# Narrow attention of two stages: unrolled program, value products of two units together, first loads issued one phase earlier

## The reference

```python
# causal, per sequence b and head h, 8 features a head, L = 1024
scores = einsum('bhqd,bhkd->bhqk', q, k) / sqrt(8)
scores = where(causal, scores, -inf)
probs  = softmax(scores, axis=-1)
o      = einsum('bhqk,bhkd->bhqd', probs, v)

# encoder block: no mask, no scaling; the bias enters outside the softmax
att     = softmax(einsum('nqd,nkd->nqk', qm, km), axis=-1)
att_out = einsum('nqk,nkd->nqd', att + batch_pos, vm)
```

## Time and profile before

| | us |
|---|---|
| three executions | 2846.60, 2834.06, 2837.32 |
| median | 2837.32 |
| the profiled execution, its own time | 2839.78 |
| its span in the trace | 2837.9 |

### The profile page before, as it was taken

The page is one execution under the profiler, slowest core; times in us unless marked ns, Lnnn a source line. Parts: engine busy times, 40 slices in busy tenths (PEclk is TensorE's granted clock), DMA queues, the critical chain, the costliest instruction groups (busy, mean ns, idle before and its releaser), DMA issues. The chain is left out here.

```text
span 2837.9 us, 41505 instructions
## 1 busy us (share of the span) xinstructions
PE 2460.7 (87%) x12171; PEld 1456.0 (51%) x12236; DVE 2092.1 (74%) x4150; ACT 1431.1 (50%) x3040; POOL 616.5 (22%) x605
## 2 busy tenths in 40 slices
PE   6994989949988999789996499999848899969998
PEld 4773344327756555467773422222225555437776
DVE  4984777538968999279995088788437899739998
ACT  3552456615522777146664026666711377616665
POOL 2324001013326000124444100000003400013443
PEclk7996899969979999789996669999978999979999
DMA  1213232022212000034432621211033000004443
GB/s 64 83 54 80 51 66 58 13 55 88 76 38 49 1 1 1 8 130 142 156 138 48 153 46 28 54 29 29 5 48 82 5 1 1 8 9 156 149 149 118
DMA packets 110480, 175.28 MB, mean 62 GB/s; under 512 B 58739, under 2 KB 81139, under 8 KB 98467
## 3 DMA queue, kind: packets, MB, share of 16 engines
q1 hardware_dynamic: 93428, 171.23, 20.6%
q10 hardware_dynamic: 16896, 2.10, 0.5%
HBM read 145.43 MB, written 12.78 MB: 56 GB/s over the span
## 5 line engine op out<-in xcount | busy, mean ns | idle before, releaser
L1543 DVE TENSOR_REDUCE b1x_maxima<-b1x_m_bank 128x1 f32<-128x512 f32 x512 | 318.1, 684 | 85.7 <-PE b1x_m_bank L1461 85.6
L1583 ACT ACTIVATE b1x_probs<-b1x_e_bank 128x1024 f32<-128x1024 f32 x256 | 248.4, 1021 | 119.9 <-PE b1x_e_bank L1479 111.6
L1543 DVE TENSOR_REDUCE a1x_maxima<-a1x_m_bank 128x1 f32<-128x512 f32 (+3 forms) x384 | 190.1, 551 | 72.6 <-PE a1x_m_bank L1464 48.6
L1461 PE MATMUL b1x_m_bank<-b1a_k_slot,b1a_q_slot 96*128 96x512 bf16 x512 | 191.4, 414 | 21.2 <-DMA b1x_v_slot<-b1a_v_aug 20.1
L1583 ACT ACTIVATE a1x_probs<-a1x_e_bank 128x1024 f32<-128x1024 f32 (+1 forms) x192 | 147.5, 809 | 103.4 <-PE a1x_e_bank L1482 80.1
L1479 PE MATMUL b1x_e_bank<-b1a_q_slot,b1a_k_slot 128*128 128x512 bf16 x475 | 146.7, 387 | 8.3 <-issue 4.3
L1495 PE MATMUL b1x_o_bank<-b1x_probs,b1x_v_slot 128*32 128x512 f32 x1024 | 138.8, 614 | 0.7 <-ACT b1x_probs L1583 0.7
L1461 PE MATMUL a1x_m_bank<-a1a_k_slot,a1a_q_slot 96*128 96x512 bf16 (+3 forms) x384 | 120.5, 352 | 18.3 <-DMA a1x_v_slot<-a1a_v_aug 16.7
L1461 PEld LDWEIGHTS b1x_m_bank<-b1a_k_slot,b1a_q_slot 96*128 96x128 bf16 x512 | 41.7, 98 | 180.5 <-DVE b1x_maxima L1543 130.9
L632 ACT ACTIVATE g2e_high<-g2e_hidden 128x512 fp32r<-128x512 f32 x128 | 81.1, 633 | 91.7 <-DVE g2e_hidden L665 91.5
L632 ACT ACTIVATE g1e_high<-g1e_hidden 128x512 fp32r<-128x512 f32 x128 | 81.1, 633 | 91.0 <-DVE g1e_hidden L665 91.0
(11 more groups left out here) (567 smaller groups left out, 6624.6 us busy)
## 6 DMA issues: line engine op xcount, KB each, us to landing
g1e_share<-scratch_combine SPq DMA_DIRECT2D x32, 1024.0 KB, 4.9
g2e_share<-scratch_combine SPq DMA_DIRECT2D x32, 1024.0 KB, 4.8
f1e_share<-scratch_combine SPq DMA_DIRECT2D x9, 1024.0 KB, 4.8
f2e_share<-scratch_combine SPq DMA_DIRECT2D x9, 1024.0 KB, 4.9
b1e_window<-scratch_bias_table SPq DMA_DIRECT2D x16, 320.0 KB, 4.7
a1a_k_slot<-scratch_k_parts SPq DMA_DIRECT2D x24, 192.0 KB
a1a_q_slot<-scratch_q_parts SPq DMA_DIRECT2D x72, 64.0 KB
b1a_k_slot<-scratch_k_parts SPq DMA_DIRECT2D x24, 192.0 KB
```

Of the source, the lines that this page charges most:

```text
L1461: mm = pe.matmul(bank[:, 0:width], q_slot[s][0:MAX_ROW, qt // 4, hh, chunk(qt % 4, 128)], k_slot[s][0:MAX_ROW, hh, k0:k0 + width], start=T ...
L1543: dve.tensor_reduce(maxima[:, k0 // NC, col:col + 1], bank[:, 0:width], AX, ALU.max).then_inc(m_taken, 1)
L1583: act.activation(probs[g % 2][:, 2 * pair:2 * pair + 2, 0:width], e_bank[pair][:, :, 0:width], ACT.Exp, scale=scale).then_inc(exp_done, 1)
```

## The change

Five things change, in both attentions.

1. **No loops.** Every engine's program of the attention phase is written out for all 8 groups (16 query halves). The units of all groups form one list (`units`), the items another (`items`).
2. **Order on PE.** For every two units u and u+1: the four score pairs of units u+2 and u+3, an item behind each of them, a fifth item, then the value products of u and of u+1 together, then the rest of the items. `probs` has four buffers instead of two; there are still two `e_bank` and three `m_bank`.
3. **Lead and shares.** Items are dealt out by their width (`worth`, `due`) and evenly over all units, with a fixed lead: 68 items stand before the first scores in `a1x` (before: 50) and 53 in `b1x` (before: 66, turns counted). A turn stands four items behind the last maximum of its half. In `b1x` the 58 rounds with items hold 8, 8, 8 and 9 of them in turn (the last of the 58 holds 5) and 6 rounds hold none; in `a1x` a group's six rounds hold 10, 5, 10, 12, 9 and 4, and the last 8 of 48 rounds none.
4. **Loads.** Group 0 is loaded by SP in the phase before (`narrow_values`, and in `relative_bias` behind the windows' loads). A group is loaded by 6 transfers: a query part is one transfer with a broadcast source to its three places. The values are read from `v_aug` where they lie, without the copy `v_slot`. Groups 1 and 2 are both loaded at the start of the attention, ahead of the first `rows`.
5. **POOL.** The third part of the maxima is written by the subtraction itself, so a half takes four POOL instructions instead of five.

The diff, cut to its core:

```diff
+    def load(self, sp, group):
+        n, s = group * 4, group % SLOTS
+        for i in range(PARTS):
+            sp.dma_start(self.k_slot[s][24 * i:24 * i + 24, :, :],
+                         self.dram["k_parts"][n:n + 4, :, :, :].rearrange("n i d t -> (i d) n t")
+                         ).then_inc(self.slot_loaded[s], 16)
+            sp.dma_start(self.q_slot[s][24 * i:24 * i + 24, :, :, :].rearrange("r e h q -> r e (h q)"),
+                         self.dram["q_parts"][i, :, :, n:n + 4, :].rearrange("d e n q -> d e (n q)")
+                         .unsqueeze(0).to_broadcast([PARTS, HD, 2, 4 * NC])
+                         ).then_inc(self.slot_loaded[s], 16)
...
+    for half in reversed(range(HALVES)):
+        items.insert(min(last_item[half] + 4, len(items)), (half, None))
...
+    AHEAD = 2 if causal else 1
...
+    worth = [0]
+    for item in items:
+        worth.append(worth[-1] + (item[4] + 32 if item[1] is not None else 256))
+
+    def due(u):
+        if u >= NU:
+            return NI
+        lead = turn_at[AHEAD - 1] + (16 if causal else 18)
+        done, whole = (sum(unit[3] + 32 for unit in units[:u]), sum(unit[3] + 32 for unit in units))
+        aim = worth[lead] + worth[NI] * done / whole
+        return max(m for m in range(NI + 1) if worth[m] <= aim)
...
-        v_slot = [p.sb(f"v_slot{s}", [128, GRANULE_TILES, 128]) for s in range(3)]
-        probs = [p.sb(f"probs{s}", [128, 4, NC]) for s in range(2)]
+        probs = [p.sb(f"probs{s}", [128, 4, NC]) for s in range(4)]
...
+            narrow.load(sp, 1)
+            narrow.load(sp, 2)
+            for half in range(AHEAD):
+                rows(half)
+            for half in range(HALVES):
+                group = half // 2 + SLOTS - 1
+                if SLOTS <= group < GROUPS and half % 2 == 0:
+                    sp.wait_ge(pv_done, last_unit[half - 1] + 1)
+                    narrow.load(sp, group)
+                if half + AHEAD < HALVES:
+                    rows(half + AHEAD)
+                store(half)
...
+            def scores(u, pair):
...
+                if u >= 1:
+                    pe.wait_ge(exp_done, 2 * u - 1 + pair)
...
-                for g in range(NG):
-                    share = [] if last else list(m_share(g))
-                    for pair in range(2):
-                        if g + 1 < NG:
-                            scores(group, s, g + 1, pair)
-                        elif not last:
-                            scores(group + 1, next_s, 0, pair)
-                        if pair < len(share) - 1:
-                            m_item(group + 1, next_s, share[pair])
-                    values(group, s, g)
-                    for m in share[min(2, max(0, len(share) - 1)):]:
-                        m_item(group + 1, next_s, m)
+            for m in range(dues[0]):
+                first_pass(m)
+            for u in range(2):
+                for pair in range(2):
+                    scores(u, pair)
+            for u in range(0, NU, 2):
+                share = list(range(dues[u], dues[u + 2]))
+                for at in range(4):
+                    if u + 2 < NU:
+                        scores(u + 2 + at // 2, at % 2)
+                    if at < len(share):
+                        first_pass(share[at])
+                for m in share[4:5]:
+                    first_pass(m)
+                values(u)
+                values(u + 1)
+                for m in share[5:]:
+                    first_pass(m)
...
+            exponentials(0)
+            exponentials(1)
+            for u in range(1, NU, 2):
+                half = units[u][0]
+                if u + 1 < NU:
+                    exponentials(u + 1)
+                    exponentials(u + 2)
+                if u == last_unit[half]:
+                    act.wait_ge(pv_done, u + 1)
...
@@ narrow_values
+        @block.sync
+        def _(sp):
+            sp.wait_ge(narrow.stored, 16 * narrow.stores)
+            narrow.load(sp, 0)
...
@@ relative_bias
+            sp.wait_ge(narrow.stored, 16 * stores)
+            narrow.load(sp, 0)
             sp.wait_ge(out_copied, NT)
```

More of the change, by code:

```diff
@@ L1125, in __init__ @@
         self.sets = 0
+        self.slot_loaded = [phase.sem(f"slot_loaded{s}") for s in range(SLOTS)]
     def store(self, sp, dst, src, sem):
@@ L1277, in narrow_attention @@
     scale = HD ** -0.5 if causal else 1.0
-    granules = []
-    for qh in range(2):
+    HALVES = 2 * GROUPS
+    units = []
+    items = []
+    for half in range(HALVES):
+        qh = half % 2
         for kt in range(GRANULE_TILES):
@@ L1432, in _ @@
-            rows(0, 0)
-            def step(it, j, group, last):
-                if not last:
-                    rows(group + 1, (j + 1) % 3)
-            over_groups(pool, step)
-        def count(group, per, index):
-            return group * per + index
+            for half in range(HALVES):
+                into = max_parts[half % 2]
+                pool.wait_ge(m_taken, turn_at[half] + 1)
+                if half >= 2:
+                    pool.wait_ge(rows_set[half % 2], 48 * (half // 2))
+                pool.tensor_copy(into[:, 0, :], rest[:]).then_inc(cut, 1)
+                pool.wait_ge(cut, 4 * half + 1)
+                pool.tensor_tensor(rest1[:], rest[:], into[:, 0, :], ALU.subtract).then_inc(cut, 1)
+                pool.wait_ge(cut, 4 * half + 2)
+                pool.tensor_copy(into[:, 1, :], rest1[:]).then_inc(cut, 1)
+                pool.wait_ge(cut, 4 * half + 3)
+                pool.tensor_tensor(into[:, 2, :], rest1[:], into[:, 1, :], ALU.subtract).then_inc(cut, 1)
@@ L1528, in _ @@
         @block.vector
         def _(dve):
-            dve.sem_inc(m_taken, 3)
-            def m_item(group, s, m):
-                item = items[m]
-                dve.wait_ge(m_done, count(group, NM, m + 1))
-                bank = m_bank[(s * NM + m) % 3]
-                if item[0] == "turn":
-                    dve.wait_ge(cut, group * (2 * CUT) + item[1] * CUT + CUT)
+            for m in range(NI):
+                half, qt = items[m][0:2]
+                qh = half % 2
+                dve.wait_ge(m_done, m + 1)
+                bank = m_bank[m % 3]
+                if qt is None:
+                    if half >= 1:
+                        dve.wait_ge(cut, 4 * half)
@@ L1561, in _ @@
-            dve.sem_inc(cut, CUT)
-            for m in range(NM):
-                m_item(0, 0, m)
-            def step(it, j, group, last):
-                if not last:
-                    for m in range(NM):
-                        m_item(group + 1, (j + 1) % 3, m)
-            over_groups(dve, step)
+                if m == last_item[half]:
+                    cols = slice(16 * qh, 16 * qh + 16)
+                    dve.wait_ge(m_taken, m + 1)
+                    if not (causal and qh == 0):
+                        dve.tensor_tensor(maxima[:, 0, cols], maxima[:, 0, cols], maxima[:, 1, cols],
+                                          ALU.max).then_inc(compared, 1)
+                        dve.wait_ge(compared, half // 2 + 1 if causal else half + 1)
+                    dve.tensor_scalar(neg_max[:, qh, :], maxima[:, 0, cols], -1.0, None,
+                                      ALU.mult).then_inc(neg_done, 1)
@@ L1812, in relative_bias @@
         v = v_true
+        stores = narrow.stores + sum(1 if m == 1 else 2 for m, i in narrow.unstored) * HD
         @block.sync
```

223 lines of the change are left out of this document (64 added, 159 removed).

## The result

The changed kernel takes 2847.88 us, the kernel before 2831.45 (medians of 20 runs each): ratio 1.0056, 95% interval 1.0037 to 1.0075, slower by some 16 us. Ratios here leave out executions in a slower state (one of the kernel before took 3011.74 us, one of E3 7054.4). The forecast was 2827 us, faster by 10. It started from 2837.32, the median of three executions; from 2831.45 the same 10 us would give 2821, so as a time 2827 flatters the forecast by some 6 us. The time lies inside the range (2795 to 2851), on the side given a chance of 0.15.

What follows compares the result with a forecast made beforehand. DVE was taken to bound the lead and PE the middle. Starts -29.0, leads -3.4, `b1x` +21 and `a1x` +1.4 sum to -10.0 us, giving 2829.8 from the profiled 2839.78, as a median 2827; range 2795 to 2851.

Steps and rivals of the forecast that it cites:

- Starts: Openings of both attentions: group 0 loaded in the phase before, PE begins 11.8 and 17.2 us earlier, -29.0 us.
- The range's +6: Allowance at the starts: broadcast loads landing two or three us later; taken as 0, +6 us kept for the range.
- edits at nothing: Dropping the value copy, and both early loads on SP ahead of the first `rows`: priced at no time.
- One round of `b1x`: Middle of `b1x`: rounds of 6.07 us, 6.79 with nine items; first score to last value 401 against 380.0, +21.
- the 4 us put on top for late maxima: `b1x`: a half's maxima just reach the slot in time; 0.3 us for 15 halves, 4.
- PE would be 87% busy: Sign in the middle of `b1x`: PE some 87% busy instead of 96%.
- `a1x`: Middle of `a1x`: a group takes 33.7 us against 32.0; first score to last value 262.3 against 260.9, +1.4.
- Leads: Items before the first scores: `b1x` 31.3 us instead of 40.8, -9.5; `a1x` 31.3 instead of 25.2, +6.1; together -3.4.
- Items behind the values cost nothing: Rival, faster: waits for DVE, 18 us in `a1x` and 10 in `b1x`, may vanish; time 2799, chance 0.22.
- The clock falls: Rival, slower: at the two waits of each round, 1.9 us a fall; 30 falls give 2884; chance 0.08.
- Maxima arrive late: Rival, slower, in `b1x`: transfers land 1.5 us later and each of 15 halves waits; +22, 2849; chance 0.10.
- Doesn't do as it says: Rival: second unit's values cost 1.00 like the first's, and broadcast loads are late, +6; 2848; chance 0.10.

Runs made afterwards that it cites:

- E3: The changed kernel with SP waiting until load 0 has landed before issuing loads 1 and 2; ratio 1.0050 to the kernel before.
- E8: E1 with plain q transfers, loads 1 and 2 held until load 0 lands, and the mask of `a1x` ahead of load 0; ratio 0.9803 to the kernel before.
- E1: The changed kernel with value products of one unit at a time again, behind the scores of the next unit; ratio 0.9853 to the kernel before.
- E6: The changed kernel with exponentials over half the columns from the ninth unit on; body of `a1x` fell by 25.3 us to 242.9, `b1x` by 13.3 to 387.7.
- E5: The changed kernel, values still in pairs, with 1, 2, 2 and 1 items behind the four score pairs; ratio 0.9930 to the kernel before.
- E11: E8 with up to two items behind each score pair in `a1x` instead of one; ratio 0.9821 to the kernel before.
- E2: The changed kernel with q parts loaded by nine plain transfers of 8 rows instead of three broadcast ones; ratio 1.0039 to the kernel before.
- E12: E8 with the keys of load 0 in `a1x` issued from ACT; that load landed after 12.4 us instead of 12.8, one execution.

## Why the prediction was wrong

- **Starts, the step that failed.** "It should land about when the attention phase opens" had no price for the load itself. Before, 12 transfers and the value copy took 14 us in `a1x` (267.9 to 282.0) and over 18 in `b1x`. I took it that six transfers would need less than the 10 us between the last store and the phase (in `b1x` it was 8.1 this time). They need 14 with no slot load behind them and 16.8 with loads 1 and 2 there. The bytes are the same 1.2 MB in fewer transfers, and before, 1.7 MB with the value copy took no longer in `a1x`, so neither the number of transfers nor the bytes alone set the time; what does stays open beyond the few busy engines of the broadcast. The term was -29.0 and measured -13.1. E8 brings the first items 5.7 and 4.9 us nearer to the phase's first cast, 10.6 of the missing 15.9; the rest is the load's own 12 to 14 us. The range's +6 had one of the mechanisms, the broadcast (3.8 us in `b1x`). That loads 1 and 2 slow load 0, I put under "edits at nothing" without a row for it, and the mask's new place behind load 0 has no term at all.
- **One round of `b1x`, right.** 6.07 and 6.79 came out as 6.17 and 6.91, +21 as +21.1; E1 and E6 show the waits for exponentials as the cause. That the sum meets the measured one to 0.1 us is luck in part: four rounds take 25.3 us where the forecast has 25.0, some 4 us over the rounds with items, and the 4 us put on top for late maxima were hardly needed (0.8 in PE's waits). The forecast that PE would be 87% busy was off: the page counts matmuls up to modelled ends, and has 94%. The sum rested on starts of instructions and not on that.
- **`a1x`, mis-sized.** The group takes 34.7 us, not 33.7, and the body 268.2, not 262.3. E6 takes off 2.9 of a group for ACT (forecast 3.0), so the missing 1.0 is in the rest, items behind the values that wait for DVE by E5 and E11; not separated further.
- **Leads, right:** +6.1 and -9.7 against +6.1 and -9.5.
- **Unforeseen:** +2.0 behind `b1x`'s last value. The four stores there took 2.77 us to issue instead of 1.35; the cause of that, and of the rest of the 2.0, stays open.
- **Rivals.** "Items behind the values cost nothing" fell: E5 gains by moving them. "The clock falls" fell: the granted clock is 1.00 in the middle of both attentions, with two stops a round. The section "A second HAM failure mode: psum-queue depth-cycling" of the Trainium skill's page "TensorE: Matmul & The Clock Gate" is not borne out by these rows. "Maxima arrive late" cost 0.8 us in PE's waits in the changed kernel, but 15 and 17 in E5 and E6. "Doesn't do as it says" held in its half on the broadcast loads.
- The larger judgement missed was to cost the change only as a whole. By the same steps, the unrolling and later turns alone would have come out well ahead: the sum itself has the turn waits and the seam of `b1x` at 12.9 + 6.7 + 1.9 us, and for the joined values 0.67 us of waits in a round, called sure, against 0.24 saved.

## What to carry to other kernels

Before joining two steps to share a fixed cost, follow each buffer through the new round: a bank that is written twice in a round has its second write wait until the reader of the first is done, and the joined stretch leaves the engines that it doesn't feed without work (here DVE, which reads the items from three banks). Of a transfer moved ahead, price its own time, from issue to landing, from a load of the same form in the trace, and what is queued in front of it and behind it; moving the issue moves the landing by less. When a round gets shorter, recompute every lead that is counted in rounds.

## What the runs showed of the hardware

- A broadcast load already issued is slowed by loads issued behind it: load 0 of `b1x` landed after 15.9 to 17.2 us with loads 1 and 2 behind it (eight kernels) and after 14.0 without (E3). In the form of nine plain transfers it took 13.0 with them (E2) and 12.1 to 13.5 without (E8, E12), so no effect shows.
- A load whose outer dimension is a broadcast of three keeps few DMA engines busy at its end: a share of 0.19 (E3), against 0.67 with plain transfers (E8).
- Issues themselves slow down when broadcast loads stand in the queue: of the twelve of loads 1 and 2, from the eighth on in `a1x` and from the fifth on in `b1x` each takes 1.0 to 4.3 us instead of 0.4 to 0.8. With plain ones (E2, `a1x`) they stay at 0.4 to 0.7.
- A mask of 128 KB lands in 2.1 us ahead of a load (the kernel before), in 9.5 behind one with two more following (the changed kernel), and in 6.1 behind one with none following (E3).
- From the first value matmul to the next item it is 1.85 us for two units' values in a row (8 matmuls) and 1.00 for one unit's (4): 0.15 saved for two.
